# A graph layer with eight experts: the router keeps its weights in TensorE, a matrix of zeros and ones sums and turns the logits, and the softmax moves one round later

## What is computed

```python
w = softmax(X @ Wr + br)                      # Wr is 256 x 8: the router
h = relu(bn1(X @ W1[e] + b1[e]))              # for each of 8 experts e, 256 x 256
h = relu(bn2(h @ W2[e] + b2[e]))
y = h @ Wo[e] + bo[e]
out = x2 + sum over e of w[:, e] * y
```

## Time and profile before

| | us |
|---|---|
| median of 3 runs | 1119.76 |
| lowest and highest | 1119.03, 1121.68 |
| the profiled execution | 1122.0 |
| its span, first to last instruction | 1120.2 |
| TensorE matmul busy | 1099.8 (98%) |
| TensorE weight load busy | 984.4 (88%) |
| VectorE busy | 771.7 (69%) |
| ScalarE busy | 715.7 (64%) |
| GpSimd busy | 246.1 (22%) |

### The profile page before, as it was taken

How to read it: one execution, slowest core, us unless ns; L and a number is a source line. 1 busy time by engine, 2 the same in 40 slices (tenths; PEclk the granted TensorE clock), 3 DMA queues, 4 the chain that set the end, 5 groups by cost and what they waited for, 6 DMA issues and landing times.

```text
span 1120.2 us, 19541 instructions
## 1 busy us (share of the span) xinstructions
PE 1099.8 (98%) x6694; PEld 984.4 (88%) x6694; DVE 771.7 (69%) x1931; ACT 715.7 (64%) x1223; POOL 246.1 (22%) x267
## 2 busy tenths in 40 slices
PE   8999998999999999999999999999999999999998
PEld 6878897888888888888888898888888988888998
DVE  7877855867576586685775865866758658667564
ACT  4776764676656665656656656666566566566665
POOL 3777764302103012021030120120300202100000
PEclk9999999999999999999999999999999999999999
DMA  5799963111011011110110110111101101100000
GB/s 163 195 239 243 259 163 102 55 32 49 11 38 58 1 48 48 39 32 27 38 58 1 48 48 20 30 48 39 53 6 44 53 1 43 34 20 1 1 20 15
DMA packets 78568, 67.83 MB, mean 61 GB/s; under 512 B 27908, under 2 KB 73846, under 8 KB 78470
## 3 DMA queue, kind: packets, MB, share of 16 engines
q1 hardware_dynamic: 73958, 59.48, 19.1%
q0 software_dynamic: 3968, 6.61, 2.4%
q10 hardware_dynamic: 543, 0.51, 0.3%
HBM read 40.77 MB, written 25.80 MB: 59 GB/s over the span
## 4 chain that ended last, share of the span: by engine, by line
PE 86%; DMA 4%; DVE 3%; issue 2%; POOL 2%; ACT 1%; SPq 1%; DVEq 0%; ACTq 0%; POOLq 0%
PE bank L271 27%; PE bank L273 27%; PE bank L272 27%; DMA weight_stage<-in_L_ffn_W 2%; PE bank L1033 1%; PE bank L1045 1%; PE bank L1043 1%; POOL gathered L569 1%; PE bank L889 1%; PE bank L1061 1%; DMA accumulated<-in_L_mix_w_qkv 1%; DMA node_alpha_l<-gathered 1%; SPq L433 0%; DMA weight_stage<-in_L_ffn_Wo 0%; PE bank L835 0%
## 5 line engine op out<-in xcount | busy, mean ns | idle before, releaser
L1261 DVE SCALAR_TENSOR_TENSOR accumulated<-bank,router_w,accumulated 128x256 f32<-128x256 f32 (+2 forms) x392 | 170.3, 479 | 199.9 <-PE bank L273 190.1
L613 ACT ACTIVATE h<-weight_stage 128x512 fp32r<-128x512 f32 (+2 forms) x206 | 113.6, 599 | 203.8 <-PE bank L273 182.8
L273 PE MATMUL bank<-ffn_w_high,h 128*128 128x256 f32 (+2 forms) x778 | 220.0, 283 | 0.0
L272 PE MATMUL bank<-ffn_w_low,h 128*128 128x256 f32 (+2 forms) x778 | 219.9, 283 | 0.0
L271 PE MATMUL bank<-ffn_w_high,h 128*128 128x256 f32 (+2 forms) x778 | 219.7, 282 | 0.0
L739 ACT ACTIVATE activated<-bank,bn_cols 128x512 f32<-128x512 f32 (+2 forms) x208 | 156.7, 753 | 56.7 <-PE bank L273 51.0
L739 ACT ACTIVATE weight_stage<-bank,bn_cols 128x512 f32<-128x512 f32 (+2 forms) x208 | 155.4, 750 | 53.9 <-PE bank L273 53.6
L1109 DVE TENSOR_TENSOR h_low<-activated,h_high 128x512 fp32r<-128x512 f32 (+2 forms) x209 | 135.0, 657 | 78.2 <-ACT h_high L613 75.1
L584 POOL DMA_INDIRECT gathered<-node_table,indices x49 | 64.1, 1309 | 528.7 <-DVE residual L1318 513.8
L271 PE MATMUL bank<-xT_high,ffn_w_high 128*128 128x512 f32 (+2 forms) x416 | 159.6, 384 | 0.4 <-DVE xT_low L1109 0.4
L271 PE MATMUL bank<-h_high,ffn_w_high 128*128 128x512 f32 (+2 forms) x416 | 157.8, 379 | 1.8 <-DVE h_low L1109 1.8
(11 more groups left out here) (204 smaller groups left out, 1884.1 us busy)
## 6 DMA issues: line engine op xcount, KB each, us to landing
x_rows<-in_x SPq DMA_DIRECT2D x18, 512.0 KB, 5.0
x_turned<-xT_high SPq DMA_DIRECT2D x22, 256.0 KB, 4.9
x_turned<-xT_low SPq DMA_DIRECT2D x22, 256.0 KB, 5.3
mix_xT_high<-x_turned SPq DMA_DIRECT2D x11, 512.0 KB
mix_xT_low<-x_turned SPq DMA_DIRECT2D x11, 512.0 KB
out<-accumulated SPq DMA_DIRECT2D x11, 512.0 KB, 3.3
weight_stage<-in_L_ffn_W SPq DMA_DIRECT2D x16, 256.0 KB, 5.0
node_table<-gathered SPq DMA_DIRECT2D x22, 130.0 KB, 4.6
```

Source lines behind the costliest of these rows:

```text
L272: nc.tensor.matmul(dst, ah, bl, start=False, stop=False)
L273: last = nc.tensor.matmul(dst, al, bh, start=False, stop=(k == n - 1))
L613: return nc.scalar.activation(dst, src, ACT.Copy)
L1261: last = V.scalar_tensor_tensor(a, Yb[b][0:tp, (t % 2) * D:(t % 2 + 1) * D], wts(ch)[0:tp, t, e:e + 1], a, ALU.mult, ALU.add)
```

## The change

The router's operands change places. Its weights `wr2` are now the stationary operand (16 and 8 columns of the array), and the turned rows stream, up to 512 at a time: four matmuls for a chunk. The output has the 16 sums of a row on partitions and the rows along the free dimension. ScalarE copies it to SBUF as fp32 (`router_rows`, into `rT`, a part of `activated` that this stage does not use). A new TensorE step `router_sum` multiplies, for each tile, these 16 x 128 values (stationary, fp32) with `pick`, a 16 x 8 fp32 matrix of zeros and ones: that adds the two halves of the columns and puts rows back on partitions. VectorE's `route` then needs three operations instead of four.

`router` stays in round 6, with `router_rows` in ScalarE's slot of that round. `router_sum`, `router_exp` and `route` go to round 7. In the first chunk `router_turn`, ScalarE's `router_turned` and VectorE's `add_bias` move to round 1, and `weights` into round 0. `pick` is made once by GpSimd out of the identity.

```diff
+        rT = tmp[0:2 * NE, 2, :]
+        pick = sb("router_pick", [2 * NE, NE])
 # GpSimd, set up
+            pool.wait_ge(s["id"], 2)
+            nc.gpsimd.tensor_tensor(pick[:, :], ident[0:2 * NE, 0:NE], ident[0:2 * NE, NE:2 * NE], ALU.add).then_inc(s["pick"], 1)
 # ScalarE
+            def router_rows(ch):
+                need(act, s["frT"], ch.c + 1)
+                need(act, s["frt"], ch.c)
+                copy(rT[:, 0:ch.rows], Fb[0][0:2 * NE, 0:ch.rows]).then_inc(s["frE"], 1)
-            FRONT = {1: gnn_exp, 2: gelu, 5: x2_high, 6: router_exp}
+            FRONT = {1: gnn_exp, 2: gelu, 5: x2_high, 6: router_rows}
-            router_exp(CHUNKS[0])
+            router_rows(CHUNKS[0])
                     elif nxt is not None:
                         relu1(nxt, 0)
-                    if e == 0 and ch.c > 0:
+                        router_exp(nxt)
+                    if e == 0 and ch.c == 0:
+                        router_exp(ch)
+                    if e == (0 if ch.c > 0 else 1):
                         router_turned(ch)
                     relu2(ch, e)
-                    if e == 0 and ch.c == 0:
-                        router_turned(ch)
 # TensorE
             def router(ch):
+                R = ch.rows
+                need(pe, s["f2lo"], KT * (ch.c + 1))
+                for k in range(KT):
+                    nc.tensor.matmul(Fb[0][0:2 * NE, 0:R], wr2[:, k, :], xTh[:, ch.par, k, 0:R], start=(k == 0), stop=False)
+                for k in range(KT):
+                    last = nc.tensor.matmul(Fb[0][0:NE, 0:R], wr2[:, k, 0:NE], xTl[:, ch.par, k, 0:R], start=False, stop=(k == KT - 1))
+                last.then_inc(s["frT"], 1)
+            def router_sum(ch):
                 tp = ch.tp
-                need(pe, s["f2lo"], KT * (ch.c + 1))
+                need(pe, s["frE"], ch.c + 1)
+                pe.wait_ge(s["pick"], 1)
                 for t in range(ch.nt):
-                    cols = slice(t * tp, (t + 1) * tp)
-                    dst = Fb[0][0:tp, 2 * t * NE:2 * (t + 1) * NE]
-                    for k in range(KT):
-                        nc.tensor.matmul(dst, xTh[:, ch.par, k, cols], wr2[:, k, :], start=(k == 0), stop=False)
-                    for k in range(KT):
-                        last = nc.tensor.matmul(dst[:, 0:NE], xTl[:, ch.par, k, cols], wr2[:, k, 0:NE],
-                                                start=False, stop=(k == KT - 1))
+                    last = nc.tensor.matmul(Fb[1][0:tp, t * NE:(t + 1) * NE], rT[:, t * tp:(t + 1) * tp], pick[:, :],
+                                            start=True, stop=True)
                 last.then_inc(s["frt"], 1)
                     elif nxt is not None:
                         L1(nxt, 0)
-                    if e == 0 and ch.c > 0:
+                        router_sum(nxt)
+                    if e == 0 and ch.c == 0:
+                        router_sum(ch)
+                    if e == (0 if ch.c > 0 else 1):
                         router_turn(ch)
                     L2(ch, e)
-                    if ch.c == 0:
-                        if e == 0:
-                            router_turn(ch)
-                        elif e == 1:
-                            out_bias(ch)
+                    if ch.c == 0 and e == 1:
+                        out_bias(ch)
 # VectorE
-                parts = Fb[0][0:tp, 0:2 * nt * NE].rearrange("p (t e) -> p t e", e=2 * NE)
-                sm.step(V.tensor_tensor(a, parts[:, :, 0:NE], brbc[0:tp, :].unsqueeze(1).broadcast_to([tp, nt, NE]), ALU.add))
-                sm.step(V.tensor_tensor(a, parts[:, :, NE:2 * NE], a, ALU.add))
+                parts = Fb[1][0:tp, 0:nt * NE].rearrange("p (t e) -> p t e", e=NE)
+                sm.step(V.tensor_tensor(a, parts, brbc[0:tp, :].unsqueeze(1).broadcast_to([tp, nt, NE]), ALU.add))
-            weights(CHUNKS[0])
                     elif nxt is not None:
                         hid1(nxt, 0)
+                        route(nxt)
                     if ch.last and e == NE - 1:
                         hid2(ch, e)
+                    if e == 0 and ch.c == 0:
+                        weights(ch)
+                    if e == 1 and ch.c == 0:
+                        add_bias(ch)
                     if e > 0:
                         accumulate(ch, e - 1)
...
-                    if e == 0:
+                    if e == 0 and ch.c > 0:
                         add_bias(ch)
```

More of the change, by code:

```diff
@@ L201, in build @@
         L1b, L2b, Yb, Fb = bank[0:2], bank[2:4], bank[4:6], bank[6:8]
-        names = """ld_b ld_w0 ld_w1 ld_g ld_bn ld_w1m ld_bo ld_small id ones eps set_pool w_sum bias_row kv_w kv_mean kv_w2 kv_hi kv_lo
+        names = """ld_b ld_w0 ld_w1 ld_g ld_bn ld_w1m ld_bo ld_small id ones pick eps set_pool w_sum bias_row kv_w kv_mean kv_w2 kv_hi kv_lo
             g_mean g_w g_prod g_sum g_hi g_lo
@@ L207, in build @@
             m_blk m_sum m_t m_kv m_p m_pv m_pa m_m m_hi m_lo m_c m_cb w1_sum w1_ev b1_new wq_sum bq_new
-            rsl xB0 xB1 xst0 xst1 xst2 xm fxn gmsg gln fm1 gelu fmh fm2 fx2 fst frs fx2n f2T f2hi f2lo frt flg fex fw3 fw3T fw3c fbo fai
+            rsl xB0 xB1 xst0 xst1 xst2 xm fxn gmsg gln fm1 gelu fmh fm2 fx2 fst frs fx2n f2T f2hi f2lo frT frE frt flg fex fw3 fw3T fw3c fbo fai
             idx0 idx1 gath0 gath1 glog gexp dsm
@@ L1266, in wts @@
                 return wpar[ch.par]
-            smalls = {"logits": 3, "messages": 7, "x2": 1, "route": 3, "weights": 4}
+            smalls = {"logits": 3, "messages": 7, "x2": 1, "route": 2, "weights": 4}
             OFF, PER = {}, 0
@@ L1399, in add_bias @@
                     V.tensor_tensor(a, a, Fb[b][0:tp, 0:(t1_ - t0) * D].rearrange("p (t d) -> p t d", d=D), ALU.add).then_inc(s["fai"], 1)
-            FRONT = {0: (base_rows, logits), 1: (messages,), 2: (gel_split,), 3: (x2,), 4: (x2_norm,), 5: (x2_low,), 6: (route,)}
+            FRONT = {0: (base_rows, logits), 1: (messages,), 2: (gel_split,), 3: (x2,), 4: (x2_norm,), 5: (x2_low,)}
             md = Chain(dve, s["m_t"])
```

## The result

The changed kernel has a median of 1124.85 us over 11 runs (1121.23 to 1128.43), the kernel before beside it 1119.05 over 11 (1117.67 to 1121.68). The ratio is 1.0049, 95% interval 1.0038 to 1.0061: slower by half a per cent. The forecast was 1123.2 us, in ratio 1.003.

What follows compares the result with a forecast made beforehand. TensorE bounds the kernel. Per 512-row chunk 0.92 + 1.17 - 1.79 = +0.30 us; eleven give +3.3, last chunk +0.28, first chunk -0.2: +3.4 on 1119.76 gives 1123.2 us, range 1117.6 to 1127.0.

Steps and rivals of the forecast that it cites:

- The removed 1.79: TensorE, each 512-row chunk: the old router's 16 matmuls cost 1.79 us, 0.112 each, and go away.
- the streaming router: TensorE, each 512-row chunk: four 512-column matmuls at 0.23 us add 0.92 us, their narrow loads hidden.
- Rival 1: Streaming router: narrow columns empty the array too, at most another 0.3 us a chunk, 1126.8 us in all; chance 0.13.
- the change of rows: Around `router_sum` on TensorE: going from 128 rows to 16 and back adds 0.27 us a chunk, bounds 0 and 0.38.
- the eight loads: In `router_sum`: four plain fp32 calls are two loads each, 0.112 us a load, 0.90 us a chunk.
- Rival 2: `router_sum` is cheap, one load a call and nothing emptied: 0.53 us, -0.34 a chunk, 1115.7 us in all; chance 0.07.
- Rival 3: `router_sum` has two loads a call but nothing emptied: 0.90 us, +0.03 a chunk, no change at 1120 us; chance 0.12.
- The covers: Slack of ScalarE and VectorE: 1.7 us ahead of the sum, 1.3 before the high copies, 0.5 on VectorE; no new waits.
- The two new waits: First chunk: TensorE waits some 0.9 us for the turn's input and 0.7 for ScalarE's copy ahead of `out_bias`.
- the 1.16: First chunk: TensorE's 1.16 us wait for VectorE's low parts was to nearly go.
- the 0.65: First chunk: TensorE's second wait for VectorE's low parts, 0.65 us, was to stay, with VectorE 0.2 us early.

Runs made afterwards that it cites:

- e2: Changed kernel with `router_sum` on all 128 rows of the array instead of 16: 75.69 us a chunk against 75.94; 1121.26 us in one execution.
- e1: Changed kernel with every call of `router_sum` made twice (eight calls instead of four): 76.85 and 76.84 us a chunk against 75.94; 1133.4 us in one execution.
- e3: Changed kernel with four fp32 transposes in place of the sum's products, VectorE adding the halves: 1112.25 us, ratio 0.9951 to the kernel before; 75.27 us a chunk.
- e5: The changed kernel measured again without edit: 1122.42 us over 10 runs beside 1118.59 for the kernel before, ratio 1.0030.
- e7: Changed kernel with `router_sum`, exponential and VectorE's part back in round 6, the sum directly behind the router: 1141.93 us in one execution.

## Why the prediction was right

**The bound** was read rightly: PE stays busy in every chunk, and all that it gained or lost arrived in the time.

**The removed 1.79 and the streaming router.** For the streaming router 0.92 was forecast, 0.94 measured. The narrow loads hide, and the array does not empty at 16 columns: the load starts at 601.17 under the matmul ahead. Rival 1 falls by that line. The Trainium skill (TensorEngine Tiling (Array Packing), Key Properties) says that a switch between tile modes drains the array; by these traces it holds for the change of rows (e2: 0.26 us) and not for that of columns (0.94 us for four matmuls, where any four of 512 columns take 0.92). Whether a load of 16 columns counts as a change of mode at all, the traces don't say.

**`router_sum`.** 1.17 forecast, 1.18 measured, and both terms hold by themselves: e1 measures the eight loads (0.90 forecast, 0.90), e2 the change of rows (0.27 forecast, 0.26). Rival 2 had a single load for each call and no emptying; e1 and e2 speak against both, and e3 shows that the halved price does exist, for transposes. Rival 3 falls by e2: the emptying is there.

**A chunk and the total.** +0.30 forecast, +0.34 measured; eleven chunks give 3.8 us where I had 3.3. The last chunk has its share. The total was forecast at +3.4, the traces have +3.9 and +3.0 from the first L1 on, and the medians +5.8 and +3.8. The intervals of the two measurements overlap from 1.0038 to 1.0041. The first lies some 2 us above what its trace explains. Without its four executions at a clock of 0.994 or 0.995 it is +4.5 (e5), so the clock has a share in it; the rest, and why the clock fell, stay open. The chunks were forecast for the right reasons; the first chunk's share was luck, as shown below.

**ScalarE and VectorE.** The covers are there as I had them, or longer. In the timeline of ACT in the changed kernel:

```profile
602.61 0.57 ACT L617 ACTIVATE activated<-bank 16x512 f32<-16x512 f32 x1
...
606.62 1.28 ACT L802 ACT_TABLE_LOAD   x1
607.91 0.23 ACT L802 ACTIVATE router_logits<-router_logits 128x32 f32<-128x32 f32 x1
608.05 0.76 ACT L743 ACTIVATE weight_stage<-bank,bn_cols 128x512 f32<-128x512 f32 x1
...
612.02 1.15 ACT L617 ACTIVATE h<-weight_stage 128x512 fp32r<-128x512 f32 x2 [2.15 <-PE bank L275]
```

The rows are out at 603.2, 1.9 us ahead of the sum (1.7 forecast). The table load and the exponential are done at 608.1, and ScalarE still stands 2.15 us before the high copies (I had 1.3 of cover), so the late ReLUs cost nothing. e7 is the other side of it: without the L1 in between, 0.85 us of wait appear at once.

**The first chunk.** From the first L1 to the first turn of a next chunk: 35.83 us before, 35.67 in the changed kernel's trace, 34.81 in its second one: -0.2 and -1.0, where I had -0.2. The two new waits stand where I put them (0.9 and 0.7 us), in the timeline of PE:

```profile
192.71 0.29 PE L1070 MATMUL bank<-identity,router_w 120*64 120x120 f32 x1 [0.81 <-issue]
195.79 0.49 PE L1079 MATMUL bank<-bo_rows,router_wT 64*120 64x512 f32 x1 [1.40 <-ACT router_wT L617]
```

and the two waits of PE in the earlier trace rows, the 1.16 and the 0.65, are gone. I had the 0.65 still in place; VectorE was far enough ahead. In the second trace the 1.40 is 0.46; ScalarE stood for 0.54 us between the two in the first trace and did not in the second, which explains some half of the difference. So the -0.2 of the first trace is luck: a wait twice as long as forecast and one that did not come cancel each other.

## What to carry to other kernels

Exchange stationary and moving operand only with the whole bill in hand. Here it saved twelve small matmuls and brought four plain fp32 products, each with two loads of 128 stationary columns, on 16 rows of the array between stretches on 128: read what a small matmul costs from the distances between starts around one that is already in the trace, count the loads and not the calls, and look at the load before and behind for a gap. Then pay once: four tiles stacked on partitions 0, 32, 64 and 96 need one product in place of four, on the full height, and that turned +0.34 us a chunk into -0.59. And a consumer put behind its producer with other work between them is worth more than the wait, if the wait can bring the clock down (e7).

## What the runs showed of the hardware

- With 8 columns streamed, the loads of plain fp32 products follow each other at 0.11 us, with 16 partitions or with 128 (e1, e2), as those of float32r products with 128 partitions do. The loads of transposes of 16 partitions follow each other at 0.06 (e3); with 128 columns streamed, transposes too stand 0.11 apart.
- A change from 128 rows to 16 and back costs 0.26 us beyond the loads (e2), with short matmuls in between; how much of it falls on the way in and how much on the way out, no run separates. A change to 16 and 8 columns costs nothing that shows.
- A wait of 0.85 us with eight short matmuls behind it was followed in six of ten cases by a fall of the granted clock to 0.50 that began 1.5 us after full work had resumed and cost 1.64 us (e7). In the changed kernel, with no such wait, no chunk shows one in either trace.
